# A reordered scan stage: tanh ahead of root and late weights on ScalarE, one moved step each on GpSimd, VectorE and TensorE

## The reference

```
h    = rmsnorm(x) * norm_w;  proj = h @ in_proj_w.T          # gate, hidden, B, C, dt
hBC  = silu(causal_conv(hBC, conv_w, conv_b))                # 4 taps
M    = (C @ B.T) * exp(segsum(A*dt));  Y_diag = M @ (hid*dt) # chunks of 128 rows
Y_off = C @ carried_state * exp(cumsum(A*dt))
yg   = (Y_diag + Y_off + D*hid) * silu(gate)
y    = rmsnorm over each group of 1024 of yg, * gnorm_w;  out = residual + y @ out_proj_w.T
```

## Time and profile before

| | before |
|---|---|
| median of 3 runs | 1997.73 us (1997.22 to 1998.42) |
| profiled execution, its own time | 2001.5 us |
| its span | 1999.6 us |
| TensorE busy | 1926.9 us, 96% of the span |
| ScalarE / VectorE / GpSimd busy | 80% / 77% / 76% |
| granted TensorE clock, mean | 0.996 of full speed |

### The profile page before, as it was taken

One profiled execution on the slowest core, in us unless ns is written; L12 is line 12 of the kernel. 1 busy time (PEld: TensorE's weight loads), 2 busy tenths in 40 slices (PEclk: granted clock), 3 DMA queues, 4 the chain that ended last, 5 costly groups with the idle time before them and its releaser, 6 DMA issues.

```text
span 1999.6 us, 32828 instructions
## 1 busy us (share of the span) xinstructions
PE 1926.9 (96%) x10675; PEld 1548.9 (77%) x10675; DVE 1540.3 (77%) x2806; ACT 1609.5 (80%) x3244; POOL 1523.4 (76%) x1114
## 2 busy tenths in 40 slices
PE   8999999999999999999999999999999999999998
PEld 6574667777888888888888878787878888888876
DVE  8787898866777777777777777777777878787878
ACT  5354866657898989898989898989888888888886
POOL 5644778647787878787878787878787787878887
PEclk9999999999999999999999999999999999999999
DMA  5625323543333333434333343434343434343333
GB/s 203 195 68 140 100 89 110 163 166 116 119 106 122 103 122 104 127 99 126 110 115 120 106 126 100 134 101 130 104 124 104 130 100 126 109 153 117 118 107 122
DMA packets 114474, 241.74 MB, mean 121 GB/s; under 512 B 23681, under 2 KB 24706, under 8 KB 113794
## 3 DMA queue, kind: packets, MB, share of 16 engines
q1 hardware_dynamic: 110466, 227.06, 36.7%
q0 software_dynamic: 3840, 12.59, 2.2%
HBM read 226.75 MB, written 12.85 MB: 120 GB/s over the span
## 4 chain that ended last, share of the span: by engine, by line
PE 28%; ACT 20%; DVE 13%; POOL 11%; issue 7%; DMA 1%; SPq 0%; ACTq 0%; DVEq 0%; POOLq 0%
PE ps L75 7%; PE ps L76 6%; PE ps L77 6%; POOL w_lo L2710 6%; ACT s_lm L2214 5%; PE ps L2129 4%; DVE s_cv L2457 3%; ACT s_scale L2237 3%; ACT s_cv L2247 2%; ACT s_hid L2281 2%; PE ps L2137 2%; POOL s_y_lo L2741 2%; DVE xs L2502 2%; POOL s_ssq L2720 2%; DVE s_hdt L2445 2%
## 5 line engine op out<-in xcount | busy, mean ns | idle before, releaser
L75 PE MATMUL ps<-h_hi,w_hi 128*128 128x512 f32 x1168 | 471.7, 404 | 13.5 <-POOL w_lo L2710 8.6
L2710 POOL TENSOR_TENSOR w_lo<-w_raw,w_hi 128x1024 fp32r<-128x1024 f32 x142 | 337.8, 2387 | 186.5 <-ACT w_hi L2197 186.5
L2457 DVE SCALAR_TENSOR_TENSOR s_cv<-ps,s_par,s_cv 128x511 f32<-128x511 f32 (+2 forms) x480 | 359.1, 748 | 128.3 <-ACT s_cv L2247 117.1
L76 PE MATMUL ps<-h_lo,w_hi 128*128 128x512 f32 x1168 | 456.0, 390 | 0.0
L77 PE MATMUL ps<-h_hi,w_lo 128*128 128x512 f32 x1152 | 450.9, 391 | 0.0
L2214 ACT ACTIVATE s_lm<-s_rows,s_steps 128x128 f32<-128x128 f32 x1024 | 324.0, 389 | 24.6 <-PE ps L2129 24.6
L2736 POOL TENSOR_TENSOR s_lm<-s_lm,s_cbt 128x512 f32<-128x512 f32 x256 | 327.8, 1307 | 14.4 <-ACT s_lm L2229 11.9
L75 PEld LDWEIGHTS ps<-h_hi,w_hi 128*128 128x128 f32 x1168 | 219.6, 188 | 68.1 <-DVE s_hid L2465 23.2
L77 PEld LDWEIGHTS ps<-h_hi,w_lo 128*128 128x128 f32 x1152 | 216.3, 188 | 47.1
L76 PEld LDWEIGHTS ps<-h_lo,w_hi 128*128 128x128 f32 x1168 | 220.1, 188 | 41.3 <-issue 0.2
L2741 POOL TENSOR_TENSOR s_y_lo<-s_hid,s_y_hi 128x512 fp32r<-128x512 f32 x120 | 155.7, 1298 | 66.4 <-ACT s_hid L2281 66.4
(11 more groups left out here) (338 smaller groups left out, 4464.6 us busy)
## 6 DMA issues: line engine op xcount, KB each, us to landing
w_raw<-in_w_in SPq DMA_DIRECT2D x144, 512.0 KB, 3.7
s_rows<-acs_dram SPq DMA_DIRECT2D x256, 256.0 KB, 3.6
s_wo_raw<-in_w_out SPq DMA_DIRECT2D x128, 256.0 KB, 3.2
w_raw<-in_gu_q SPq DMA_DIRECT2D x14, 512.0 KB, 3.6
f_d_q<-in_d_q SPq DMA_DIRECT2D x28, 256.0 KB, 2.7
f_d_w<-in_d_s SPq DMA_DIRECT2D x28, 256.0 KB, 3.7
table<-shifted SPq DMA_DIRECT2D x16, 256.0 KB, 2.6
xs<-in_x SPq DMA_DIRECT2D x8, 256.0 KB, 6.1
```

Source lines behind the costliest of these rows:

```text
L75: nc.tensor.matmul(dst, l_hi, r_hi, start=start, stop=False)
L76: nc.tensor.matmul(dst, l_hi, r_lo, start=False, stop=False)
L2457: nc.vector.scalar_tensor_tensor(dst, src[:, 0:SEQ - d], par[:, v.b, 4 * j + 3 - d:4 * j + 4 - d], dst, ALU.mult, ALU.add).then_inc(conv_c ...
L2710: nc.gpsimd.tensor_tensor(w_lo[:, slot, :], w_raw[:, slot, :], w_hi[:, slot, :].bitcast(F32), ALU.subtract).then_inc(w_lo_ready, 1)
```

## The change

Five moves, with no operation added, removed or resized:

- ScalarE, doubles 0, 2 and 3: tile b's tanh goes from the end of the double to between the two `act_scale` pairs, ahead of the second pair and the late weight block. In double 3 the late block also goes ahead of the root (`act_rms`).
- ScalarE, double 1: tile b's tanh goes ahead of C's tap, which goes ahead of the scales of tile a.
- VectorE, double 1: tile b's silu goes ahead of the state recurrence.
- GpSimd, double 1: the low part of the block with B and C goes ahead of tile b's sum of squares.
- TensorE, double 2: `CB` goes behind `OP_1` of tile a.

```
 double_jobs:
     else:
+        if s == 3:
+            jobs += [(A_BANK, ("SQ", 0, 0))]
+        jobs += [one]
         if s == 2:
             jobs += [(A_BANK, ("CB", 1, 0))]
-        if s == 3:
-            jobs += [(A_BANK, ("SQ", 0, 0))]
-        jobs += [one, *both, two]
+        jobs += [*both, two]
 act_double:
             act_exps(act, ub, b_on)
-            act_scale(act, ua, a_on)
             if s == 1:
                 c_bank, b_bank = bank(un, ("H", 1, C_AT)), bank(un, ("H", 1, B_AT))
+                act_tanh(act, v, tile_of(b), h_b)
                 act_tap(act, v, C_AT, c_bank)
-                act_tanh(act, v, tile_of(b), h_b)
+                act_scale(act, ua, a_on)
                 act_scale(act, ub, b_on)
                 act_w(act, *load_unit(un, LATE[s]))
...
                 return
+            act_scale(act, ua, a_on)
+            act_tanh(act, v, tile_of(b), h_b)
             act_scale(act, ub, b_on)
+            if load_unit(un, LATE[s]):
+                act_w(act, *load_unit(un, LATE[s]))
             if s == 3:
                 act_rms(act, un)
-            if load_unit(un, LATE[s]):
-                act_w(act, *load_unit(un, LATE[s]))
-            act_tanh(act, v, tile_of(b), h_b)
 dve_double:
                 dve_tile(dve, v, tile_of(b), h[1])
+                dve_silu(dve, v, tile_of(b), h[1])
                 state()
-                dve_silu(dve, v, tile_of(b), h[1])
 pool_double:
             pool_y_lo(pool, un, b)
-            pool_sum(pool, un, b)
             if s == 1:
                 pool_w(pool, v, LOADS.index(("BC", 0)))
+            pool_sum(pool, un, b)
```

## The result

| | before | after |
|---|---|---|
| median | 1997.5 us (4 runs, 1997.2 to 1998.4) | 2013.7 us (4 runs, 2013.5 to 2016.3) |
| ratio, 95% interval | | 1.0083 (1.0066 to 1.0101) |
| profiled execution, its own time | 2001.5 us | 2016.25 us |
| its span | 1999.6 us | 2014.4 us |
| granted TensorE clock, mean | 0.996 | 0.991 |

What follows compares the result with a forecast made beforehand. TensorE, busy 96% of the span, was taken to bound the kernel. Fourteen steady units at +0.1 gave +1.4 us, unit 0 +0.7, unit 15 -1: together +1.1, 1998.8 us on the median, 8 in 10 range 1985 to 2009.

Steps and rivals of the forecast that it cites:

- an exchange of three stalls for one at block 2: Stalls at double 0's DIAG b (1.43), H C_AT (0.73), CB (0.77) go; about 2.4 us appears before double 1's G; chance 0.53.
- every sign named for it: L2253's load gone, 15 at L2260; ScalarE idle 2.9, TensorE 2.2; none at H C_AT, CB; period within 0.3 of 98.1.
- Sum: TensorE's shifts added over a steady unit: +0.1 us; with units 0 and 15, +1.1 us in all.
- `DIAG` b of double 2: TensorE, double 2: wants to start at 110.5, starts at 110.63 because B's silu frees its bank late; +0.13 a unit.
- shift ahead of block 2: TensorE after double 0: -0.65, as DIAG b of double 1 stands behind tile 1's silu, only 0.65 earlier.
- price of block 2: Double 0's moved tanh makes weight block 2 late for double 1's first G: +2.46, leaving TensorE's shift at +1.81.
- nothing that is waited for: GpSimd, double 1: moving the sum behind B and C's low part delays nothing needed; ST's low inputs follow at 98.56, needed 98.8.
- the delay of double 1 isn't healed in double 2: Slower rival: VectorE and ScalarE enter double 2 1.2 us late, unit keeps +0.5 to +1, 2008 us; chance 0.20.
- three places that it named: ST's low inputs, CB, and block 7's low part, counted as having 0.3 to 0.5 us of slack.
- The last unit's 1 us: Unit 15 has only the win of the earlier tanh before it: 1 us taken of 1.43, bounds 0 and 1.43.
- The one with block 2 not in the way: Faster rival: stalls go, block 2 isn't late, -1.5 a unit, 1976 us; half of it 1980 to 1993; together 0.24.
- The one with a drain: Slower rival: the table switch costs a drain too, double 0's gate 1.36 later, +1.4 a unit, 2017 us; chance 0.03.

Runs made afterwards that it cites:

- the kernel with double 1 undone: Changed kernel with double 0's tanh back, tanh behind the root ahead of the last unit, and double 1's old order on VectorE and ScalarE: ratio 0.9882.
- GpSimd as before: Changed kernel with double 0's tanh back, tanh behind the root ahead of the last unit, and GpSimd's move undone: ratio 0.9870.
- Filling the stall: Changed kernel plus nine extra fp32r products, results overwritten, ahead of the first G of double 1: 2018.4 us, ratio 1.0052.
- shortening it to 1.21: Changed kernel with double 0's tanh behind the second scale pair, ahead of the late block: 2001.6 us, ratio 0.9969.
- `CB` alone: Kernel before with one part of the change, CB behind OP_1 of tile a in double 2: ratio 0.9933.
- double 3, 1 or 0 alone: Kernel before with only that double's moves (double 3: ScalarE's; double 1: all three; double 0: the tanh): ratios 0.9971, 1.0014, 1.0221.
- double 0 alone: Kernel before with only double 0's tanh moved between the two scale pairs: 2049.8 us, ratio 1.0221.

## Why the prediction was wrong

The picture was right: the change is an exchange of three stalls for one at block 2, and every sign named for it showed (the load gone from the tanh, 14 at the gate and one at the last unit's scale, ScalarE idle 2.94 ahead of the tanh, TensorE idle 2.29 ended by L2712, none at `H C_AT` and `CB`). Wrong was the step **Sum**, with its +0.1 a unit and +1.1 in all, against +14.8 between the two spans. Two of its terms failed most: the fall of the clock, which it put at nothing, measured 7.8 us, and `DIAG` b of double 2, put at 0.13 a unit, measured 0.52.

| step of the prediction | forecast | measured |
|---|---|---|
| double 0: y, gate, tanh behind `OFF` | 4.69, 8.27, 23.61 | 4.69, 8.38, 23.70 |
| shift ahead of block 2 | -0.65 | -0.55 (`T` 26.10 against 26.65) |
| price of block 2; shift behind it | +2.46; +1.81 | +2.53; +1.98 (29.05 against 27.07) |
| `H C_AT` and `H B_AT` | -1.07 | -1.10 (shift +0.88) |
| `DIAG` b of double 2 | +0.13 | +0.52 (shift +1.40) |
| `CB` | -0.77 | -0.89 |
| a steady unit | +0.1 | +0.52 |
| fall of the clock | none | 1.3 in 6 of 15 |
| unit 14 | +0.1 | +0.5, +1.25, and its fall |
| last unit | -1 | -0.05 |

Times behind `OFF` are of the unit at 962.20, so y is 966.89 - 962.20. The shifts compare the same matmul in the units of 1055.67 and 962.20.

**The ring terms.** Each was right to 0.2 us but one: `DIAG` b of double 2, mis-sized by 0.39, which is all but the whole of the unit's 0.42. I had it start at 110.63, 54.96 behind the unit's `OFF`, just behind the end of B's silu; it started at 55.49, and the silu at 54.75, for 0.69. VectorE's timeline after, and GpSimd's:

```profile
1009.95 0.43 DVE L2485 TENSOR_SCALAR gu_s<-s_par 128x8 f32<-128x8 f32 x1
...
1016.95 0.69 DVE L2467 SCALAR_TENSOR_TENSOR s_bT<-ps,s_cv 128x512 f32<-128x512 f32 x1 [0.67 <-ACT ps L2254]
```

```profile
1005.28 5.07 POOL L2738 TENSOR_TENSOR s_lm<-s_lm,s_cbt 128x512 f32<-128x512 f32 x4
```

Of the 0.53 by which `DIAG` b is late, 0.14 came in with the shift. Another 0.27 is the small operation behind the states (L2485), which took 0.43 here where it took 0.16 before. It ends with GpSimd's product: at 1010.38, where the last of the four ends at 1010.35, and 0.03 us behind the product then running in each of the 15 units. The same in the kernel with double 1 undone, where it took 0.73 (VectorE, then GpSimd):

```profile
996.34 0.73 DVE L2489 TENSOR_SCALAR gu_s<-s_par 128x8 f32<-128x8 f32 x1
```

```profile
992.00 5.04 POOL L2742 TENSOR_TENSOR s_lm<-s_lm,s_cbt 128x512 f32<-128x512 f32 x4
```

In all nine traces with GpSimd's moved step it took 0.23 to 0.74 us, in all seven without it 0.16 to 0.17, also where nothing but that step differs (`GpSimd as before` in the table above: 0.16 against 0.25). So VectorE waits here for GpSimd, and the step of the prediction that the move of the sum costs "nothing that is waited for" is where 0.27 of the 0.39 went missing. What the two engines share in this is shown by no run, and the last 0.1 isn't attributed. Over 14 units the term is 5.5 us. The prediction had said that 0.3 us a unit decides, in the rival *the delay of double 1 isn't healed in double 2*. That rival would have said 2008 and has the steady unit without the clock right (+0.5), though not by one of the three places that it named.

**The clock.** The step that failed by most is one that isn't in the text: that a stall costs only its length. Both ways of moving 2 us of idle time were counted as equal, three short pieces or one long one. They are not: 6 x 1.3 = 7.8 us. Filling the stall and shortening it to 1.21 each took the falls away. The earlier trace rows shows a clock of 1.00 with stalls up to 1.20. A steady unit had no longer stall that could have warned; the last unit had (1.67 and 1.84), with a fall behind them in one of two traces.

**The ends of the scan.** The last unit's 1 us was cancelled by the table load, which here goes ahead of whatever next needs the other table; I followed it for the steady unit and not for the last, where scales and not a gate come next. Leaving that tanh behind the root gave 2.0, 1.3 of it by the earlier y. Unit 14's 1.25 was not seen: its GpSimd has two more operations. By the distance of unit 14 over that of unit 13 (without falls) it is 0.9 to 1.3 us in every kernel with both double 3's order and that of `CB`, 0.4 with `CB` alone, and nothing with double 3, 1 or 0 alone. It isn't a matter of a shorter period: at 97.55 there is none, at 97.53 there is 1.26. What joins the two was not isolated.

These terms together: 14 x 0.52 + 1.1 (unit 0 without its fall) + 7.8 + 1.25 - 0.05 - 2.6 (the head) = 14.8, the difference of the spans.

**The rivals.** The one with block 2 not in the way is out. The one with a drain is out too: its 2017 is near the measured time, but for another reason. The load at 969.29 ends at 970.57 and the gate starts at 970.58. The Trainium skill (ScalarE: Activation LUTs, "What ACT_TABLE_LOAD costs") puts about 1380 ns of drain on top; no load of the root's or the gate's in these traces shows it: the function follows within 0.02 us, except at the very last root, which waits for VectorE. Taking both loads out won 0.88 us by the one steady unit without a fall (98.62 to 97.74), less than one load's 1.28.

**Open.** Why the same 2.29 to 2.31 us of idle time brings the clock down in 6 of 15 units of the changed kernel, 9 with double 0 alone, and 13 without the table loads. The two traces of the changed kernel agree in the number and not in which units, and the last unit of the kernel before fell in one trace of two, so it isn't the unit's work. Open too are what joins double 3's order and that of `CB` in unit 14, and the last 0.1 of `DIAG` b.

## What to carry to other kernels

When an instruction is moved up on an in-order engine, list what now stands behind its wait and follow both ways from it to the bound engine: a stall that is the difference of two ways out of one instruction can't be shortened by anything upstream of it. Price one long stall of TensorE above several short ones of the same sum, and look at the granted clock behind it before calling an exchange even. When an instruction moves on GpSimd, look at what VectorE runs at the same time, also where no semaphore joins the two. Try the parts of a reordering alone: here the orders of double 3 and of `CB` carry 1.44 of the 1.56 us won, double 0's costs 2.08 a unit, and without that one the same patch is 0.9% faster (0.9909) instead of 0.8% slower.

## What the runs showed that I had not expected

- A stall of 2.3 us in a TensorE that is otherwise busy for 96% of the time was at times followed by a lower granted clock (mean 0.72 in a window of 6 us from there), costing 1.3 us, and 0.8 where another stall stood behind to swallow part. Single stalls of 1.2 us were not, in 14 units of each trace of the kernel before and in all 15 of the one with the tanh behind the pair; two of 1.67 and 1.84 close together were in one trace of two.
- A small operation of VectorE stretched from 0.16 to as much as 0.74 us, to end 0.03 us behind the product that GpSimd was running, though in the program it waits only for a load.
- With the root's function exchanged for one without a table load, the unit won less than the load: the gate came 1.41 us earlier (8.38 to 6.97 behind `OFF`), but the tanh behind it only 0.84 and the period 0.88.
- The stretch ahead of the scan, with the same instructions, varies by 12 us between executions (465.0 to 477.1). Steady units of one trace without a fall lie within 0.15 us of each other, and their mean was 98.10 in both traces of the kernel before. That makes the period the better measure for parts worth under 0.2%.
